# Batch 0's rope factors from a table product instead of a gather, in a fused four-layer attention kernel; steps and banks in a new order

## What is computed

```
cos = cos_t[pos][:, None]
sin = sin_t[pos][:, None]
return x * cos + _rotate_half(x) * sin
```

## Time and profile before

| what | value |
|---|---|
| three timed runs | 299.94, 300.79, 304.99 us (median 300.79) |
| the profiled execution, its time | 301.38 us |
| its span in the profile | 299.6 us |
| mean granted TensorE clock | 0.978 |
| instructions | 8817 |

### The profile page before, as it was taken

How to read it: one execution, slowest core, us unless ns; L and a number is a source line. 1 busy time by engine, 2 the same in 40 slices (tenths; PEclk the granted TensorE clock), 3 DMA queues, 4 the chain that set the end, 5 groups by cost and what they waited for, 6 DMA issues and landing times.

```text
span 299.6 us, 8817 instructions
## 1 busy us (share of the span) xinstructions
PE 260.2 (87%) x3104; PEld 158.4 (53%) x3104; DVE 241.9 (81%) x561; ACT 235.4 (79%) x522; POOL 173.8 (58%) x274
## 2 busy tenths in 40 slices
PE   4275987899898888998888999999989999999983
PEld 3263543455565666666656766575444545445542
DVE  4179998999487897798889388998999999998912
ACT  1232456799998786598899998998989899898991
POOL 7778759347796667665482878856455654620000
PEclk9999799999999997899999999999999999999997
DMA  6678654211232232133231213212221213030001
GB/s 175 202 190 214 153 163 118 64 49 46 64 91 58 75 98 73 49 83 89 72 89 28 72 40 80 73 36 59 55 68 42 74 51 80 22 102 26 21 3 35
DMA packets 40619, 23.81 MB, mean 79 GB/s; under 512 B 4856, under 2 KB 39680, under 8 KB 40448
## 3 DMA queue, kind: packets, MB, share of 16 engines
q1 hardware_dynamic: 37264, 19.30, 24.7%
q10 hardware_dynamic: 3056, 3.83, 4.8%
q0 software_dynamic: 256, 0.13, 0.2%
HBM read 6.64 MB, written 0.54 MB: 24 GB/s over the span
## 4 chain that ended last, share of the span: by engine, by line
PE 45%; DVE 21%; DMA 9%; ACT 8%; SPq 7%; issue 7%; ACTq 1%; POOL 1%; DVEq 0%; POOLq 0%
PE ps L700 27%; DVE neg_max L1111 14%; PE ps_heads L700 13%; SPq L493 6%; DMA q_stack<-q_parts 5%; ACT probs L925 3%; DMA q_stack<-max_rows 2%; PE ps L875 2%; DMA rope_rows<-in_rope,pos_row 1%; PE ps L879 1%; SPq L574 1%; DVE stats L1071 1%; DMA pos_i<-in_pos 1%; ACTq L493 1%; ACT hidden L1043 1%
## 5 line engine op out<-in xcount | busy, mean ns | idle before, releaser
L1111 DVE TENSOR_REDUCE neg_max<-ps 128x2 f32<-128x512 f32 (+1 forms) x256 | 158.6, 682 | 9.4 <-PE ps L700 8.8
L925 ACT ACTIVATE probs<-ps 128x512 f32<-128x512 f32 x256 | 134.8, 626 | 10.4 <-PE ps L700 9.8
L700 PE MATMUL ps_heads<-probs,v_cols 128*32 128x256 f32 (+1 forms) x1280 | 76.9, 348 | 2.5 <-ACT probs L925 1.5
L700 PE MATMUL ps<-k_stack,q_stack 62*128 62x256 bf16 (+1 forms) x640 | 66.0, 255 | 5.9 <-DMA q_stack<-q_parts 5.1
L700 PE MATMUL ps<-q_stack,k_stack 64*128 64x256 bf16 (+1 forms) x640 | 66.0, 254 | 1.8 <-DMA q_stack<-max_rows 1.4
L700 PEld LDWEIGHTS ps<-k_stack,q_stack 62*128 62x128 bf16 x640 | 33.1, 96 | 28.1 <-issue 7.9
L700 PEld LDWEIGHTS ps<-q_stack,k_stack 64*128 64x128 bf16 x640 | 33.6, 96 | 24.3 <-issue 8.8
L700 PEld LDWEIGHTS ps_heads<-probs,v_cols 128*32 128x32 f32 x1280 | 31.9, 110 | 26.5 <-issue 11.1
L676 POOL TENSOR_TENSOR rstd<-var_eps,minus_half 128x2 f32<-128x2 f32 x20 | 14.1, 705 | 37.3 <-DVE var_eps L1077 37.3
L700 PE MATMUL ps<-src_t,w 128*128 128x256 f32 x96 | 29.6, 425 | 2.2 <-issue 1.1
L476 POOL TENSOR_TENSOR k_parts<-q_f,k_parts 128x256 bf16<-128x256 f32 x20 | 13.4, 669 | 28.6 <-issue 25.0
(11 more groups left out here) (117 smaller groups left out, 381.8 us busy)
## 6 DMA issues: line engine op xcount, KB each, us to landing
k_stack<-k_parts SPq DMA_DIRECT2D x120, 64.0 KB, 2.1
q_stack<-q_parts SPq DMA_DIRECT2D x114, 64.0 KB, 2.1
w<-in_w ACTq DMA_DIRECT2D x3, 512.0 KB, 5.0
gates<-gate_row SPq DMA_DIRECT2D x1, 1536.0 KB, 6.7
rows<-in_rows ACTq DMA_DIRECT2D x1, 704.0 KB, 4.8
w<-in_w ACTq DMA_DIRECT2D x1, 576.0 KB, 5.0
q_stack<-max_rows SPq DMA_DIRECT2D x36, 8.0 KB
ctx_t<-in_ctx_t SPq DMA_DIRECT2D x4, 128.0 KB, 2.5
```

What stands on the lines that cost most here:

```text
L700: return nc.tensor.matmul(out, lhs_t, rhs, start=start, stop=stop, **k)
L925: nc.scalar.activation(probs[:, n % PROB_BUFS, :], ps[bank[st]][:, :], ACT.Exp, scale=SCALE).then_inc(exped, 1)
L1111: nc.vector.tensor_reduce(dst, src, AX.X, ALU.max, negate=True).then_inc(max_taken, 1)
```

## The change

Batch 0 no longer gathers. Its 256 position numbers are sent to all partitions (`first_i`, 128 x 256 integers), and the whole rope table is loaded with four rows in each partition, their row numbers behind them (`table`, 128 x 132). DVE makes the row numbers and four matrices of ones and zeros, `picks` (in the memory of `hidden`, which the MLP uses later): one where the token's row is the partition's i-th row. ACT widens the table (`table_wide`, two instructions of 128 x 512). PE then multiplies: `ps_heads` gets four fp32 products for cos and four for sin, each 128 x 128 by 128 x 256. They stand behind both projections, where the four transposes stood.

```diff
-            act.dma_start(pos_i[:, :], a["pos"]).then_inc(pos_loaded, 16)
+            act.dma_start(first_i[:, :], a["pos_first"].partition_broadcast(P)).then_inc(first_loaded, 16)
             act.dma_start(c_t[:, :], a["c_t"]).then_inc(c_loaded, 16)
+            act.dma_start(table[:, :], a["table"]).then_inc(table_loaded, 16)
+            act.dma_start(pos_i[:, :], a["pos"]).then_inc(pos_loaded, 16)
...
+            act.wait_ge(table_loaded, 16)
+            for i in range(0, PICKS, 2):
+                nc.scalar.activation(table_wide[:, i:i + 2, :, :].rearrange("p n f (r e) -> p (n f r) e", e=PAIRS),
+                                     table[:, i * ROPE_COLS:(i + 2) * ROPE_COLS].unsqueeze(2)
+                                     .broadcast_to([P, 2 * ROPE_COLS, PAIRS]), ACT.Copy).then_inc(table_expanded, 1)
...
+            def pick_rows():
+
+                dve.wait_ge(first_loaded, 16)
+                low, p, row = (first_f[:, i, :] for i in range(3))
+                link(nc.vector.tensor_scalar(low, first_i[:, :], 0.0, float(MAX_POS), ALU.is_lt, ALU.mult))
+                link(nc.vector.tensor_tensor(p, first_i[:, :], low, ALU.add))
+                link(nc.vector.tensor_scalar(row, p, 0.0, float(MAX_POS - 1), ALU.max, ALU.min))
+                dve.wait_ge(table_loaded, 16)
+                for i in range(PICKS):
+                    at = PICKS * ROPE_COLS + i
+                    nc.vector.tensor_scalar(picks[:, i, :], row, table[:, at:at + 1], None, ALU.is_equal).then_inc(picked, 1)
...
+                        for f in range(2):
+                            for i in range(PICKS):
+                                if f == 0:
+                                    pe.wait_ge(table_expanded, i // 2 + 1)
+                                    pe.wait_ge(picked, i + 1)
+                                last = mm(ps_heads[:, f * T:(f + 1) * T], table_wide[:, i, f, :], picks[:, i, :],
+                                          start=(i == 0), stop=(i == PICKS - 1))
+                        last.then_inc(rope_turned, 1)
                         pe.wait_ge(const_loaded, 16)
+                        continue
...
-                        sp.wait_ge(gathered[0], NT * 16)
+                        sp.wait_ge(gathered[1], NT * 16)
...
-    return "act" if (kind, u) == ("q", 0) else "sp"
+    return "act" if (kind, u) == ("q", 0) and part < 2 else "sp"
...
-    "HLHLLLLLRRPLRPDPSDHSDRDPSPGGRmmDmmLSPmmmHmmDXLRDPmTmDPGRmSmmmYmPmRXsmsPmSmssGTPmmsDmDvYvmssmsmmssmLDvmssDmmvssmXsvmmmm"
+    "LHLHLLRLLRPLSRDPLDHRDSDPPPGSDmRSmDmDRmmmmmGXHmGmPmmTDPPmmRYPsLsmSmmsXmRsmmsSmLTPGsmmmmsDvDmmmsYmvvsDmsDmsmXvmsmssmvFTs"
```

More of the change, by code:

```diff
@@ L480, in split, with place_parts @@
             engine.wait_ge(*third)
-        def place_parts(engine, kind, u, rest):
+        def place_parts(engine, name, kind, u, rest):
             buf = u % STACK_BUFS
+            mine = [part for part in (range(1, PARTS) if rest else (0,)) if placer(kind, u, part) == name]
+            if not mine:
+                return
             if u < STACK_BUFS:
@@ L936, in _ @@
                         load_w(act, name)
[L937 removed]
+                elif st[0] == "expand" and st[1]:
                     b = st[1]
```

69 lines of the change are left out of this document (41 added, 28 removed).

## The result

| | before | changed |
|---|---|---|
| median of 22 timed executions each | 301.40 us (297.85 to 307.14) | 304.48 us (302.19 to 311.20) |
| ratio, 95% interval | | 1.0111 (1.0084 to 1.0138) |
| the profiled execution, its time and span | 301.38, 299.6 us | 303.46, 301.7 us |
| mean granted TensorE clock there | 0.978 | 0.968 |
| instructions | 8817 | 8853 |

The change makes the kernel 1.1% slower. I had forecast 299.0 us, 0.6% faster, with a range up to 302.3: the forecast and its range were wrong. The difference is under the 2% that the prediction called "about what a measurement of this kernel can tell from no change", but 22 executions each tell it from nothing.

A forecast was written before the change was run, and what follows sets the result against it. Bound: the gather up to 13.9 us, DMA issues up to 23.8, PE with ACT and DVE after 60. Gains 1.0 + 0.3 + 0.5 = 1.8 us gave a median of 299.0 us, range 296.0 to 302.3.

The forecast's parts named there:

- The product: PE, behind the projections: eight fp32 products priced at 5.0 us, mostly at the full clock rate, ready at 13.1 us.
- DVE's picks: DVE at the start: three chained instructions and four compares, 2.6 us from 3.9 to 6.5 us, hidden by the projections.
- "I take 0.3" for the loads ahead of the projections: Kernel head: 128 + 66 KB more loads delay the projections by 0.3 us, at most 0.6; PE free at 8.1.
- SP's wait for batch 1's gather: SP's queue: the gather lands at 13.8 us, SP is free for k at 15.6, so the rope's lead is lost there.
- SP's wait decides: Rival, SP's queue: a gather landing at 16.0 delays k's DMAs, landing 0.9 us later than before; 301.7 us, chance 0.15.
- "I take 0.3" for the 512 KB ahead of q: Before unit 0's q stack DMAs: the weight load travelling ahead costs 0.3 us, between nothing and 1.5 us.
- The DMA queue gives it back: Rival, DMA at the start: 0.7 MB more before the first max costs 2.1 us, about the lead; 300.8 us, chance 0.17.
- First score, 0.3 us: Before 60 us: the first score stands behind 14 max products and not 17, 0.3 us gained (0 to 1.8).
- The rest, 0.5 us won: After the first score: the new order wins 0.5 us of PE's 15.2 us of idle, ends -1.5 to +3.5.
- all that comes after it is shifted by what it gains or loses: Premise on 0 to 24 us: the start is a latency, so its gain or loss moves everything later.

The follow-up runs named there:

- numbers_alone: The kernel before with only the position numbers added, broadcast to all partitions at the head of ACT's queue (128 KB, unused); timed once, 303.79 us.
- both_mended: w12_as_before with the two new loads third and fourth on ACT's queue and the gather's row numbers made ahead of the picks; ratio 1.0024.
- w12_early: The kernel before with one letter moved: the 512 KB weight load issued ahead of unit 0's q stack DMAs; ratio 1.0191.
- after_filled_short: The changed kernel with 14 identity products, read by nobody, on TensorE ahead of unit 0's first max; ratio 1.0088.
- w12_late: The changed kernel with the second weight load (512 KB) directly behind unit 0's q stack DMAs; ratio 1.0112.
- rope_loads_behind: The changed code with both order strings of the kernel before, the two new loads third and fourth on ACT's queue and the row numbers first; ratio 1.0102.
- w12_as_before: The changed kernel with the second weight load back in its old place, behind batch 2's widening; ratio 1.0035.
- batches_late: both_mended with the loads of batches 2 and 3 behind unit 0's stack DMAs on SP; ratio 1.0034.
- late_filled: batches_late with unread identity products ahead of batch 1's transposes and the first max of units 0, 9 and 11; ratio 0.9999.

## Why the prediction was wrong

- *The product.* The mechanism was right and the price too high: the projections of q and k and the product are one unbroken run, and the product took 3.65 us against my 5.0, nearly all of it at the full rate (sixteen records in 3.65 us, where four of the projections took 1.91). The Trainium skill, "TensorE: Matmul & The Clock Gate", section "Part 1: The HAM clock gate", says that sustained activity releases the low rate; the trace agrees. The product took 3.62 to 4.90 us in the variants, so the point at which the rate rose moves. The rope came at 13.22, forecast 13.1; that it fits so well is luck, since the product began 1.4 us late (9.46 against 8.1) and was 1.4 us cheap.
- *DVE's picks.* Forecast 2.6 us, measured 2.26 (5.59 to 7.85). They started 1.7 us later than my 3.9, with the load, and ended 0.35 past my upper end, still hidden by the projections.
- *"I take 0.3" for the loads ahead of the projections.* Failed: 1.87 us (5.91 against 4.04). I had priced it by bytes at 334 GB/s; numbers_alone shows that one broadcast of 128 KB costs 1.7 us by itself. The product, cheaper than forecast, made up for it at the rope.
- *SP's wait for batch 1's gather.* Loads at 13.63 and k from 15.50, forecast 13.8 and 15.6: right, and both_mended confirms that this wait eats the rope's lead. The rival "SP's wait decides" did not happen.
- *"I take 0.3" for the 512 KB ahead of q.* This is the step that failed first and most: I had 0 to 1.5 us, and q's last landing was 6.90 us instead of 2.99, 3.9 us more. My bound "at 334 GB/s 1.5 us of transfer at most" went by bytes at a rate read in one microsecond; at 22 to 25 us, with q on its way, the engines moved 203 to 231 GB/s at a share over 1.1. w12_early gives the term alone: 2.9 us at the landing, 3.0 at the end of the profiled span, 3.4 to 8.1 in the timed executions. So unit 0 was complete at 26.41, not at 22.3, and the start lost 2.8 us at the first max where 1.0 was to be gained.
- *The rival "The DMA queue gives it back"* came nearest: it had bytes on the DMA queue cost 2.1 us, at the peak rate again, and so no gain; at the first max it was a loss. The rule that it cited (the Trainium skill, "DMA: Bandwidth & Descriptors", section "Queues, rings and completion order") would hold back ACT's own five DMAs of q; no row of the changed kernel shows when these landed. The one that PE waited for stood on SP's queue, behind no weight load, and was late all the same, which ring order alone does not give. In after_filled_short, which has the same queues, the five on ACT's queue took 6.5 us to landing (median) and the one on SP's 6.5 as well, so both queues were held up alike. In w12_late, where that load stands behind all of ACT's q DMAs, SP's still took 4.34 us.
- *First score, 0.3 us.* From first max to first score 11.09 us instead of 12.32: 1.2 us gained, more than forecast. It is why the first score is only 1.6 us late. At unit 11 the changed kernel is 2.7 us late again.
- *The rest, 0.5 us won.* Failed in sign. From the first score on the mended orders lose what they had won: 1.6 to 3.9 us at 32 to 35 us are down to 0.5 us ahead to 1.6 us behind at unit 11, and bring nothing at the end. So the prediction's premise that "all that comes after it is shifted by what it gains or loses" failed too: one loss (w12_early) was carried through its profile, no gain was, and rope_loads_behind lost 3.0 us with a start that was not late.

## What to carry to other kernels

Before a DMA that others wait for, count what travels on the DMA engines at that time on any queue, and price it by measured landings of such DMAs beside a large load, not by bytes over peak rate; one load moved one letter earlier cost at least 3 us here. Keep a broadcast load of 128 KB away from the head of the kernel when the first projections wait for loads on another queue. And count a gain at the start only once a place in the middle of the kernel is shown to have it too: five kernels here (w12_late, w12_as_before, both_mended, batches_late, late_filled) had their first score 0.8 to 3.9 us ahead and none is faster than the kernel before.
